# Causal mask added inside VectorE's row-maximum instruction instead of by a matmul, with the order of the attention steps made anew

## The reference

```python
k = apply_rope(x @ Wk.T); v = x @ Wv.T          # one key/value head of 128
q = apply_rope(einsum('btd,hkd->bhtk', x, Wq))  # two query heads
scores = einsum('bhtk,bsk->bhts', q, k) * HS ** (-0.5)
scores = where(tril(ones((T, T))), scores, -inf)   # causal, T = 1024
w = softmax(scores, axis=-1)
out = einsum('bhts,bsk->bhtk', w, v)            # then @ Wo.T, and x is added
```

## Time and profile before

| | |
|---|---|
| median of 3 runs | 813.8 us (811.59 to 818.97) |
| the profiled execution | 819.09 us |
| its span, first to last instruction | 817.1 us |
| attention phase | up to about 483 us of the span |
| mean granted TensorE clock, as a share of 2.4 GHz | 0.959 |
| busy in the span: PE, DVE, ACT, POOL | 93%, 74%, 62%, 34% |

### The profile page before, as it was taken

The page is one execution under the profiler, slowest core; times in us unless marked ns, Lnnn a source line. Parts: engine busy times, 40 slices in busy tenths (PEclk is TensorE's granted clock), DMA queues, the critical chain, the costliest instruction groups (busy, mean ns, idle before and its releaser), DMA issues. The chain is left out here.

```text
span 817.1 us, 13720 instructions
## 1 busy us (share of the span) xinstructions
PE 756.8 (93%) x4276; PEld 604.7 (74%) x4276; DVE 606.0 (74%) x1414; ACT 508.7 (62%) x1117; POOL 281.3 (34%) x360
## 2 busy tenths in 40 slices
PE   6699999999999999999999979999999999999952
PEld 4578888888888888888887867677777776676731
DVE  4578777777786786787777873778788788888664
ACT  3476567576566666665765535667667677767642
POOL 2566445454546355364543000112121111222100
PEclk9899999999999999999999998999999999999975
DMA  7000011011011101100100017001000000001001
GB/s 210 1 2 26 27 53 47 6 53 52 15 39 53 53 2 53 53 30 23 53 1 1 1 58 252 1 12 41 27 27 27 26 26 26 28 31 48 26 27 51
DMA packets 34570, 32.43 MB, mean 40 GB/s; under 512 B 3524, under 2 KB 34244, under 8 KB 34500
## 3 DMA queue, kind: packets, MB, share of 16 engines
q1 hardware_dynamic: 34500, 31.56, 12.0%
HBM read 16.88 MB, written 14.68 MB: 39 GB/s over the span
## 5 line engine op out<-in xcount | busy, mean ns | idle before, releaser
L564 DVE TENSOR_TENSOR pT_lo<-bank,pT_hi 128x512 fp32r<-128x512 f32 (+1 forms) x160 | 98.8, 631 | 43.7 <-ACT pT_hi L486 43.6
L666 DVE TENSOR_REDUCE neg_max<-scores_ps 128x1 f32<-128x256 f32 (+7 forms) x128 | 96.3, 752 | 44.8 <-PE scores_ps L800 44.0
L486 ACT ACTIVATE pT_hi<-bank 128x512 fp32r<-128x512 f32 (+1 forms) x160 | 84.9, 554 | 51.1 <-PE bank L821 47.2
L537 ACT ACTIVATE x_all<-scores_ps,neg_max 128x256 f32<-128x256 f32 (+7 forms) x128 | 95.3, 746 | 24.7 <-DVE neg_max L666 23.9
L376 POOL TENSOR_TENSOR rope_a<-x_all,cos_sb 128x384 f32<-128x384 f32 x60 | 60.7, 1011 | 139.2 <-ACT x_all L516 135.6
L1336 PE MATMUL cycle_ps<-h,w_sb 128*128 128x512 f32 x192 | 92.7, 621 | 16.4 <-ACT h L1084 16.4
L821 PE MATMUL bank<-ident,x_all 128*128 128x128 f32 x576 | 83.9, 274 | 3.5 <-DVE pT_lo L564 3.3
L217 POOL TENSOR_TENSOR f_rstd<-f_var_eps,minus_half 128x4 f32<-128x4 f32 x16 | 16.5, 1033 | 199.7 <-DVE f_var_eps L210 199.7
L1336 PEld LDWEIGHTS cycle_ps<-h,w_sb 128*128 128x128 f32 x192 | 36.2, 196 | 62.5 <-ACT h L1084 32.7
L1033 POOL TENSOR_TENSOR h_w<-h,w_sb 128x256 f32<-128x256 f32 x48 | 35.0, 729 | 116.1 <-ACT h L1098 116.1
L821 PEld LDWEIGHTS bank<-ident,x_all 128*128 128x128 f32 x576 | 65.0, 141 | 10.8 <-issue 4.1
(11 more groups left out here) (139 smaller groups left out, 1986.8 us busy)
## 6 DMA issues: line engine op xcount, KB each, us to landing
x_all<-x SPq DMA_DIRECT2D x16, 512.0 KB, 3.9
out<-x_all SPq DMA_DIRECT2D x16, 512.0 KB, 2.9
x<-x_all SPq DMA_DIRECT2D x12, 512.0 KB, 2.9
x_all<-x SPq DMA_DIRECT2D x6, 1024.0 KB, 6.5
x_all<-wqkv SPq DMA_DIRECT2D x1, 512.0 KB, 5.1
sin_sb<-sin_t SPq DMA_DIRECT2D x1, 512.0 KB, 7.0
cos_sb<-cos_t SPq DMA_DIRECT2D x1, 256.0 KB, 5.7
x_all<-wo SPq DMA_DIRECT2D x1, 256.0 KB, 5.4
```

Of the source, the lines that this page charges most:

```text
L486: return nc.scalar.activation(out, in_, ACT.Copy)
L537: nc.scalar.activation(probs[p % 2][:, r, 0:keys], scores_ps[r % 2][:, score_columns(keys)], ACT.Exp, bias=neg_max[:, p * ROWS + r:p * ROW ...
L564: return dve.tensor_tensor(out, whole, hi.bitcast(F32), ALU.subtract)
L666: dve.tensor_reduce(neg_max[:, p * ROWS + r:p * ROWS + r + 1], scores_ps[r % 2][:, score_columns(keys)], AX_X, ALU.max, negate=True).then_ ...
```

## The change

The mask product on TensorE goes away. A float32 tile `mask` of 128 x 1024 takes the place of the two bf16 tiles: zero everywhere but in its last 128 columns, where -1e30 stands above the diagonal; its last `keys` columns are the mask of a row block with `keys` keys. VectorE's maximum becomes one `tensor_tensor_reduce`: it reads the scores in PSUM and the mask in SBUF, writes minus their sum into `probs` in SBUF, and gives the minimum of that, which is the negated maximum. ScalarE then reads `probs` and writes the exponential over it in place, with scale -1. The wait for the transposes of pair p - 2 moves from ScalarE to VectorE, since VectorE now writes `probs` first. TensorE's wait for a free scores tile changes from `probs_ready` to `max_ready`. All four step lists are written anew (the sets of steps are the same, their order differs); the parts of the new lists that the text below speaks of stand in the diff.

```diff
@@ the lists, parts only
     "tensor": [
...
+        ("scores", -1, 1, 0), ("attend", -2, 3, 2), ("turn_p", -2, 3, 7), ("attend", -2, 3, 3),
+        ("scores", -1, 1, 1), ("turn_x", 0, 0, 1), ("scores", -1, 1, 2), ("attend", -2, 3, 4),
...
+        ("turn_p", -1, 0, 1), ("scores", -1, 2, 0), ("output", -2, 3, 0), ("attend", -1, 0, 0),
+        ("turn_p", -1, 1, 0), ("scores", -1, 2, 1), ("output", -2, 3, 1), ("turn_p", -1, 1, 1),
+        ("project", 0, 0, 2), ("attend", -1, 0, 1), ("turn_p", -1, 1, 2), ("scores", -1, 2, 2),
...
     "vector": [
...
-        ("turn_p", -3, 3, 3), ("turn_p", -3, 3, 4), ("scores", -2, 1, 0), ("turn_x", -1, 0, 0),
-        ("turn_x", -1, 0, 1), ("turn_p", -3, 3, 5), ("norm", -1, 0), ("turn_p", -3, 3, 6),
...
+        ("turn_p", -3, 3, 5), ("norm", -1, 0), ("turn_x", -1, 0, 0), ("scores", -2, 1, 0),
+        ("scores", -2, 1, 1), ("turn_p", -3, 3, 6), ("turn_p", -3, 3, 7), ("turn_x", -1, 0, 1),
...
+        ("turn_p", -2, 0, 1), ("output", -3, 2, 1), ("output", -3, 3, 0), ("scores", -2, 2, 0),
+        ("turn_p", -2, 1, 0), ("output", -3, 3, 1), ("scores", -2, 2, 1), ("close", -2, 0),
@@ GpSimd, constants
-            pool.memset(ident_b[:], 0.0).then_inc(zeroed, 1)
-            pool.memset(mask_b[:], 0.0).then_inc(zeroed, 1)
+            pool.memset(mask[:], 0.0).then_inc(zeroed, 1)
@@ ScalarE, scores
-                        before = (p - 2) % PAIRS
-                        at_least(act, p_turned, (b - (p < 2)) * BATCH_STEPS
-                                 + FIRST_STEP[before] + STEPS[before])
                         at_least(act, inv_ready, (b - 2) * PAIRS + p + 1)
                     nc.scalar.activation(probs[p % 2][:, r, 0:keys],
-                                         scores_ps[r % 2][:, score_columns(keys)],
-                                         ACT.Exp, bias=neg_max[:, p * ROWS + r:p * ROWS + r + 1],
+                                         probs[p % 2][:, r, 0:keys],
+                                         ACT.Exp, scale=-1.0, bias=neg_max[:, p * ROWS + r:p * ROWS + r + 1],
@@ VectorE, scores
-                    dve.tensor_reduce(neg_max[:, p * ROWS + r:p * ROWS + r + 1],
-                                      scores_ps[r % 2][:, score_columns(keys)], AX_X, ALU.max,
-                                      negate=True).then_inc(max_ready, 1)
+                    if r == 0:
+                        before = (p - 2) % PAIRS
+                        at_least(dve, p_turned, (b - (p < 2)) * BATCH_STEPS
+                                 + FIRST_STEP[before] + STEPS[before])
+                    dve.tensor_tensor_reduce(out=probs[p % 2][:, r, 0:keys],
+                                             in0=scores_ps[r % 2][:, score_columns(keys)],
+                                             in1=mask[:, T - keys:], scale=-1.0, scalar=FAR,
+                                             op0=ALU.add, op1=ALU.min,
+                                             accum_out=neg_max[:, p * ROWS + r:p * ROWS + r + 1]
+                                             ).then_inc(max_ready, 1)
@@ TensorE, scores
-                    at_least(pe, probs_ready, s - 1)
+                    at_least(pe, max_ready, s - 1)
...
-                    mm = nc.tensor.matmul(ps[:, out.stop - P:out.stop], ident_b[:], mask_b[:],
-                                          start=False, stop=True)
```

More of the change, by code:

```diff
@@ L21 @@
 MASKED = -1e30
+FAR = 3e38
 HALF = HS // 2
@@ L26 @@
 BIAS_ROWS = 33
-ZEROED = 11
+ZEROED = 10
 SLOTS = 4
@@ L58 @@
     "tensor": [
[L59 to L79, removed]
+        ("scores", -2, 3, 0), ("turn_p", -2, 2, 0), ("turn_p", -2, 2, 1), ("turn_x", -1, 1, 0),
+        ("scores", -2, 3, 1), ("turn_x", -1, 1, 1), ("attend", -2, 1, 2), ("output", -2, 0, 1),
@@ new lines @@
+        ("scores", -1, 0, 2), ("turn_p", -2, 3, 1), ("scores", -1, 0, 3), ("turn_p", -2, 3, 2),
+        ("turn_p", -2, 3, 3), ("attend", -2, 3, 0), ("turn_p", -2, 3, 4), ("attend", -2, 3, 1),
+        ("turn_p", -2, 3, 5), ("project", -1, 1, 3), ("turn_x", 0, 0, 0), ("turn_p", -2, 3, 6),
+        ("scores", -1, 1, 0), ("attend", -2, 3, 2), ("turn_p", -2, 3, 7), ("attend", -2, 3, 3),
+        ("scores", -1, 1, 1), ("turn_x", 0, 0, 1), ("scores", -1, 1, 2), ("attend", -2, 3, 4),
+        ("turn_p", -1, 0, 0), ("output", -2, 2, 0), ("scores", -1, 1, 3), ("turn_qk", -1, 1, 0),
@@ L80 @@
+        ("attend", -1, 1, 1), ("turn_p", -1, 1, 3),
     ],
     "scalar": [
[L82 to L96, removed]
+        ("project", -2, 0, 2), ("turn_p", -3, 1, 2), ("scores", -3, 2, 0), ("scores", -3, 2, 1),
+        ("scores", -3, 2, 2), ("scores", -3, 2, 3), ("project", -2, 0, 3), ("turn_p", -3, 1, 3),
@@ L97 @@
+        ("close", -2, 0), ("turn_p", -2, 1, 1),
     ],
     "vector": [
[L99 to L103, removed]
@@ L110 @@
[L110 to L114, removed]
+        ("turn_p", -3, 1, 2), ("output", -3, 0, 0), ("norm", -2, 1), ("turn_p", -3, 1, 3),
@@ new lines @@
+        ("scores", -3, 3, 0), ("rope", -2, 1), ("turn_p", -3, 2, 0), ("rope", -2, 2),
+        ("turn_p", -3, 2, 1), ("scores", -3, 3, 1), ("rope", -2, 3), ("turn_x", -2, 1, 0),
+        ("turn_x", -2, 1, 1), ("output", -3, 0, 1), ("close", -3, 1), ("turn_p", -3, 2, 2),
+        ("turn_qk", -2, 0, 0), ("scores", -3, 3, 2), ("output", -3, 1, 0), ("scores", -3, 3, 3),
+        ("turn_qk", -2, 0, 1), ("turn_p", -3, 2, 3), ("turn_p", -3, 2, 4), ("turn_qk", -2, 0, 2),
+        ("output", -3, 1, 1), ("scores", -2, 0, 0), ("scores", -2, 0, 1), ("turn_p", -3, 2, 5),
@@ L120 @@
+        ("project", -3, 0, 3), ("project", -3, 1, 0), ("project", -3, 1, 1), ("project", -3, 1, 2),
+        ("project", -3, 1, 3), ("norm", -2, 0),
     ],
```

57 lines of the change are left out of this document (39 added, 18 removed).

## The result

| | median | executions | mean granted clock |
|---|---|---|---|
| before, as first measured | 813.85 us (811.24 to 819.05) | 14 | |
| changed kernel | 811.38 us (806.54 to 813.42) | 14 | 0.960 |
| changed kernel, second set | 810.6 us | 12 | 0.9615 |
| before, beside the later experiments | 813.7 us | 99 | 0.966 |

The ratio of the means is 0.9944 (95% interval 0.9918 to 0.9971) and in the second set 0.9956 (0.9929 to 0.9983): 2 to 7 us less in the first, 1.5 to 6 in the second. The forecast was 803.7 us, 10 us less.

A forecast was written before the change was run, and what follows sets the result against it. TensorE was taken to bound the attention phase's steady stretch. Terms -9.3 - 0.7 - 0.2 + 1.1 + 1.0 - 0.5 - 1.5 = -10.1 us took 813.8 to 803.7 us; range 797 to 818, forecast's own 799 to 808.

The forecast's parts named there:

- the FFN phase: From 483 to 817 us, after attention: contains none of the changed steps, so its 334 us were left alone.
- the first batch: Start of the attention phase: +0.3 us for VectorE's instruction, -0.5 us for the earlier `norm` before the first projection.
- the rule under which the products were priced: Steady stretch: each instruction removed from TensorE shortens the period by its start distance while VectorE and ScalarE keep up.
- What bounds the kernel: Attention phase, about 50 to 440 us: TensorE is busy throughout; the period falls from 57.6 to about 56.2 us.
- The mask products: TensorE, attention phase: removal saves 0.07 or 0.12 us each, -9.3 us in the steady stretch, -0.7 us at the ends.
- The new order: TensorE's reordered list: products right behind transposes fall from 185 to 182, -0.2 us; start -0.5, hole -1.5 us.
- The hole at 447 us: TensorE's 2.03 us wait and the half clock behind it, near the attention phase's end: -1.5 us, bounds 0 and -3.5.
- VectorE's instruction: Add, write and minimum stream like the maximum; read-out 0.1 us each, hidden in the steady stretch, +1.1 us at the ends.
- The moved wait: VectorE's queue is held for the transposes of pair p - 2, tightest at pair 1: +1 us, bounds 0 and 9.
- The end: Last batch, from 440 us: 8 scores on a VectorE busy 17.17 of 21 us, +0.8 us.
- all four: Cases: TensorE stays the bound (0.60), new waits eat the saving (0.25), VectorE becomes the bound (0.10), more than forecast (0.05).
- the saving is eaten: Attention phase: new waits on VectorE's queue and longer scores-to-transposes chain cost 8 us more, 812 us; chance 0.25.

The follow-up runs named there:

- attn_after_old_start: The changed kernel without its FFN phase, first batch walked in before's order up to the first output step: 484.1 us, 2.2 less than with the new start.
- attn_after_mask_product: The changed kernel without its FFN phase, with the mask products put back on TensorE: 498.5 us, 12.3 more than without them.

## Why the prediction was wrong, point by point

Of the 10.1 us forecast the attention phase gave 7.5 (7.1 by the means), and the whole kernel 3.4 (means). Two steps failed most: the FFN phase, which was left at nothing and gave back some 3.7 us, and the first batch, counted as a gain of 0.2 us, where the new order costs 2.2. The third is the rule under which the products were priced; it is false in the old order.

- **What bounds the kernel.** Right for the steady stretch: TensorE is busy in all of it, and the period fell by 1.2 us per batch where 1.4 was counted, but from 56.3 to 55.1 us and not from 57.6 to 56.2.
- **The mask products.** The price of one, 0.07 or 0.12 us, was right (11.2 us for 128, and 10.8 in the matched traces). The step that failed is that all of it in the steady stretch would shorten the period "as long as VectorE and ScalarE keep up", taken as settled by VectorE's 77% load. Taken out alone, in the old order, they gave 5.7 us of the 10.0 counted; in the new order they are worth all of it. The share of busy time said nothing of the order in which an in-order engine gets to its work.
- **The new order.** Priced at -0.2 us for changes of kind, -0.5 for the start and -1.5 for the hole at 447 us. It was not followed through the first batch, where its list runs into GpSimd's rotation: 2.2 us in the attention phase alone (attn_after_old_start). The hole shrank from 2.03 to 1.51 us, not by 1.5. What the new order does give, once the products are gone, is 1.8 us over the old one; its price, little room for a late load of x, was in no term.
- **VectorE's instruction.** Right. The read-out is 82 ns where 0.1 us was taken, the streaming the same. The Trainium skill's rule (Vector Engine (DVE) Microarchitecture Reference, section Points that are easy to get wrong), that two non-bf16 SBUF sources halve the rate of one accumulating shape, is left untested by these runs: with one source in PSUM the row shows 680 ns for 512 columns, the full rate. The Trainium skill's note that an operation which writes out its accumulator is two instructions (VectorE: DVE Perf Modes, section Two Vector instructions with no wait between them) agrees with the trace, where the second is the read-out of 82 ns.
- **The moved wait.** Counted +1 us; it shows once, 2.2 us, on VectorE. Right in kind; what it costs TensorE wasn't measured by itself.
- **The end.** From 432 to 453 us VectorE is at 20.07 of 21 us. A charge there was in place; its size of 0.8 us was not measured by itself.
- **The FFN phase.** "I leave its 334 us alone" failed. Its code is untouched, but the mean clock of the whole execution fell from 0.966 to 0.961, and of the 7.1 us that the attention phase saves by the means 3.4 were left (814.2 and 810.8). Some 3 us of that loss are clock by the estimate above. Why the clock is lower stays open. The forecast had no rival for it: all four dealt with the attention phase. The nearest, "the saving is eaten", named 812 us with another cause; that its number came close is luck.
- **The range.** The measured 811.4 lies within 797 to 818; the own range of the forecast, 799 to 808, doesn't hold it. Before's profiled execution was one of low clock (0.959), and a sum made against its 819.1 us took stretches of half clock as fixed that differ from one execution to the next.

## What to carry to other kernels

Work taken from the engine that bounds a kernel is worth its start distance only if the other engines' lists let it move up; measure the removal alone in the old order before and after a new order is made, and walk the new order through the first period, where its producers are not yet ahead. Leaving a phase out gives a measurement several times sharper than the whole kernel (here 1 to 2 us of spread against 8). To tell a kernel's own time from what the clock takes, compare executions at the same clock; span times mean clock overstates what the clock costs. Where TensorE waits for VectorE, look at what VectorE waited for before: here it was a load. A change of 1% in one phase can be half undone in another phase whose code is the same.

## What the hardware showed that was not expected

- The same FFN code ran at a lower mean clock behind one order of the attention phase than behind another (0.960 to 0.9615 against 0.966; averages of 26 and 99 executions, with standard errors of 0.0006 and 0.0004), and with 22 small matmuls in idle gaps of 2 us it was 0.9685 behind the one and 0.967 behind the other.
- The clock fell to half at 535.8 us of before's trace while TensorE was busy, by the modelled ends, for all of the 8.5 us ahead, the last 5 of them with matmuls of one to 256 columns. Executions of one kernel have none or four such stretches in the middle of the FFN phase.
- A load of 512 KB of x took 3.2 to 3.6 us from issue to landing nine times and 5.2 to 6.1 us three times in one execution (attn_after_mask_product, behind 80 us).
- A higher mean clock is no aim in itself: 0.971 with fillers at 809.6 and 810.0 us, 0.966 and 0.962 without at 805.5 and 808.3.
- `tensor_tensor_reduce` with one source in PSUM and its result in SBUF takes as long as the plain maximum (680 against 686 ns at 512 columns), plus 82 ns.
- A filler with float32 operands and 128 columns holds TensorE for 0.23 us (38 of them in 8.65 us, two records each), against 0.14 us for one of 256 columns in the matmul type (14 of them in 1.92 us).
